# One graph layer on one core: another order of work in the head, the second round and the tail

## What is computed

```python
h = jnp.maximum(_layernorm(x, axis=-1), 0.0)
dep_emb = dep_emb_table[adj]
hi_t = h @ W1_w[:HID] + dep_emb @ W1_w[HID:] + W1_b      # rows i
hj_t = h @ W2_w[:HID] + dep_emb @ W2_w[HID:] + W2_b      # rows j
relevance = jnp.sum(hi_t * hj_t, axis=-1)
A = jax.nn.softmax(jnp.where(adj != 0, relevance, -1e9), axis=2)
h_syn = jax.nn.relu((A @ h) @ gcn_w + gcn_b)
return x + h_syn @ Wo_w + Wo_b
```

## Time and profile before

| | us |
|---|---|
| median of 3 runs | 360.76 (360.28 to 360.89) |
| the profiled execution | 359.88 |
| its span | 358.1 |
| PE busy | 346.7 |
| ACT busy, DVE busy, POOL busy | 264.9, 264.7, 175.2 |

### The profile page before, as it was taken

The page is one execution under the profiler, slowest core; times in us unless marked ns, Lnnn a source line. Parts: engine busy times, 40 slices in busy tenths (PEclk is TensorE's granted clock), DMA queues, the critical chain, the costliest instruction groups (busy, mean ns, idle before and its releaser), DMA issues.

```text
span 358.1 us, 9301 instructions
## 1 busy us (share of the span) xinstructions
PE 346.7 (97%) x3068; PEld 213.7 (60%) x3068; DVE 264.7 (74%) x664; ACT 264.9 (74%) x563; POOL 175.2 (49%) x354
## 2 busy tenths in 40 slices
PE   7999999899999999999999999999999999999985
PEld 6766565565657566565656566565756566565753
DVE  0998788686968777785968777695967777586664
ACT  2399896977787977778797877778697877755642
POOL 3067573756637182745638183745628183770000
PEclk9999999999999999999999999999999999999999
DMA  7994608965859395775759395675749383645052
GB/s 230 320 209 141 179 2 176 236 140 120 207 126 231 89 262 119 191 173 121 203 117 249 88 255 125 174 176 128 201 109 266 88 205 90 160 91 154 11 165 100
DMA packets 97000, 57.54 MB, mean 161 GB/s; under 512 B 60450, under 2 KB 96932, under 8 KB 96980
## 3 DMA queue, kind: packets, MB, share of 16 engines
q1 hardware_dynamic: 96272, 56.90, 63.8%
q10 hardware_dynamic: 644, 0.20, 0.3%
q0 software_dynamic: 64, 0.20, 0.2%
HBM read 17.44 MB, written 12.58 MB: 84 GB/s over the span
## 4 chain that ended last, share of the span: by engine, by line
PE 87%; DVE 4%; ACT 4%; DMA 2%; issue 1%; DVEq 0%; SPq 0%; ACTq 0%
PE bank L1174 24%; PE bank L1175 24%; PE bank L1176 24%; PE bank L1428 3%; PE bank L1423 3%; PE bank L1277 3%; PE bank L1285 2%; DMA x_all<-in_L_gnn_W_w_dram 2%; PE bank L1218 2%; ACT bank L652 1%; ACT h_tok L497 1%; PE bank L1488 1%; PE bank L1490 1%; ACT h_parts L497 1%; DVE bank L1069 0%
## 5 line engine op out<-in xcount | busy, mean ns | idle before, releaser
L449 POOL TENSOR_TENSOR h_parts<-h_tok,h_parts 128x1536 f16<-128x1536 f32 (+1 forms) x15 | 43.6, 2907 | 94.4 <-ACT h_parts L497 94.3
L1174 PE MATMUL bank<-gw_hi,hT 128*128 128x385 f16 x192 | 63.1, 328 | 1.6 <-DVE g_parts L924 1.1
L1176 PE MATMUL bank<-gw_hi,hT 128*128 128x385 f16 x192 | 62.7, 327 | 0.0
L425 POOL TENSOR_TENSOR x_all<-x_all,bo_all 128x1536 f32 (+1 forms) x16 | 55.0, 3442 | 15.7 <-ACT h_tok L515 15.7
L1175 PE MATMUL bank<-gw_lo,hT 128*128 128x385 f16 x192 | 62.6, 326 | 0.0
L924 DVE TENSOR_TENSOR g_parts<-bank,g_parts 128x512 f16<-128x512 f32 x48 | 33.2, 691 | 36.0 <-ACT bank L570 35.8
L1174 PE MATMUL bank<-wo_hi,z_hi 128*128 128x384 f16 x180 | 58.9, 327 | 0.5 <-DVE z_lo L1044 0.5
L1176 PE MATMUL bank<-wo_hi,z_lo 128*128 128x384 f16 x180 | 58.7, 326 | 0.0
L1175 PE MATMUL bank<-wo_lo,z_hi 128*128 128x384 f16 x180 | 58.7, 326 | 0.0
L1174 PE MATMUL bank<-hT,m_hi 128*128 128x512 f16 x144 | 54.6, 379 | 0.7 <-DVE hT L747 0.7
L1175 PE MATMUL bank<-hT,m_hi 128*128 128x512 f16 x144 | 54.6, 379 | 0.0
(11 more groups left out here) (165 smaller groups left out, 644.2 us busy)
## 6 DMA issues: line engine op xcount, KB each, us to landing
x_all<-in_x_dram SPq DMA_DIRECT2D x16, 768.0 KB, 6.9
out_dram<-x_all SPq DMA_DIRECT2D x15, 768.0 KB, 5.2
hg_parts<-hg_lo SPq DMA_DIRECT2D x32, 192.0 KB, 3.6
hg_parts<-hg_hi SPq DMA_DIRECT2D x32, 192.0 KB, 3.9
x_all<-in_L_gnn_W_w_dram SPq DMA_DIRECT2D x2, 576.0 KB, 5.2
out_dram<-x_all SPq DMA_DIRECT2D x4, 192.0 KB, 1.9
gcn_raw<-in_L_gnn_gcn_w_dram SPq DMA_DIRECT2D x1, 576.0 KB, 10.8
x_all<-in_L_gnn_Wo_w_dram SPq DMA_DIRECT2D x1, 576.0 KB, 11.5
```

Source lines behind the costliest of these rows:

```text
L425: nc.gpsimd.tensor_tensor(x_all[:, s, :, :], x_all[:, s, :, :], bo_all[:, :, :].broadcast_to([P, KT, D]), ALU.add).then_inc(x_biased, 1)
L449: ins = nc.gpsimd.tensor_tensor(h_parts[:, at, 1, :], h_tok[:, at, :], h_parts[:, at, 0, :], ALU.subtract)
L1174: nc.tensor.matmul(dst, lh, rh, start=(c == 0), stop=False)
L1176: last = nc.tensor.matmul(dst, ll, rh, start=False, stop=(c == DC - 1))
```

## The change

In the head:
- ACT copies W2 out of PSUM; before it was DVE.
- q is the 385th column in M's second and third chunk, so that one product with W1 (three matmuls) is left of two. The second chunk is made behind p and q and waits for q's copy; the bound's matmul stands behind the first matmul of the third chunk. DVE copies two columns out of M's banks.
- Three of four tiles of x(0) are normalised on DVE, one on ACT. The steps of M's scale on DVE stand one place earlier.
- gcn's bias is loaded through SP's queue behind gcn_w, before through ACT's. The broadcast of Wo's bias on POOL waits for W2.
- POOL works out x(1)'s coefficients before both bias passes, which follow one behind the other.

In the second round:
- ACT's three high parts of Wo stand behind the first move of scores, before one stood ahead of the transposed tiles. DVE's third low part of Wo stands ahead of the statistics of x(3).
- ACT splits hg's first tile between z's high part and its whole; rows are read from PSUM as soon as hg's tile is there (`row_of`), and the high parts of hg wait for them. On DVE hg's tiles 1 and 2 are split behind the two sums, tile 3 behind `exp_bias`.
- Output(1) on PE waits for z chunk by chunk.

In the tail:
- Scores go ahead of the fourth tile of hg. DVE builds three masks and a copy of the fourth's base (`last_masks`), and adds the fourth row's term to the scores later (`last_row`). The low parts of hg's tiles 2 and 3 follow `exp_bias`.
- The last attention is transposed ahead of the fourth output tile. Additions to the output of round 14 are spread: one, one, two.
- SP moves the last hg in six transfers with three waits (`move_last_hg`). The last aggregation does all products with `hg_parts` of a chunk first, then those with `hg_hi`.

The diff, cut to what the prediction speaks of:

```diff
+            def move_last_hg():
+                sp.wait_ge(z_done, DC * LAST)
+                sp.wait_ge(hg_split, KT * LAST + 2)
+                move_part(slice(0, S), hg_lo, slice(0, 2))
+                sp.wait_ge(hg_high, KT * (LAST + 1))
+                move_part(slice(S, 2 * S), hg_hi, slice(0, KT))
+                sp.wait_ge(hg_split, KT * (LAST + 1))
+                move_part(slice(0, S), hg_lo, slice(2, KT))
...
             sp.dma_start(gcn_raw[:, :, 0:D], gcn_w.rearrange("(c p) e -> p c e", p=P)).then_inc(gcn_loaded, 16)
+            sp.dma_start(gcn_raw[:, :, D:D + 1], gcn_b.rearrange("(c p o) -> p c o", p=P, o=1),
+                         allow_slow_non_contiguous=True).then_inc(gcn_b_loaded, 16)
...
+            pool.wait_ge(w2_loaded, 16)
             pool.dma_start(bo_all[:, 0, :], bo.partition_broadcast(P)).then_inc(bo_loaded, 16)
...
             add_bias(0)
-            make_bias(0)
             main_coefficients(1)
             pool.wait_ge(h_ready, 2 * KT * 2)
+            make_bias(0)
             make_bias(1)
...
+            for c in range(DC):
+                act.wait_ge(w_transposed, DC + c + 1)
+                nc.scalar.activation(w2T[:, c, 0:D], bank[DC + c][:, 0:D], ACT.Copy).then_inc(w2_copied, 1)
...
-            early_normalise(0, range(EARLY_WIDE, KT))
+            early_normalise(0, range(FIRST_WIDE, KT))
...
             def second_round():
-                wo_high_part(0)
                 for c in range(DC):
                     early_high_part(1, c)
                 move_scores(0, range(1))
-                wo_high_part(1)
-                wo_high_part(2)
+                for c in range(DC):
+                    wo_high_part(c)
...
-                z_parts(0, 0, bank[Z_BANK[0]][:, :])
+                z_high_part(0, 0, bank[Z_BANK[0]][:, :])
                 act.wait_ge(z_done, DC)
                 hg_high_part(1, 0)
-                z_parts(0, 1, bank[Z_BANK[1]][:, :])
-                z_parts(0, 2, bank[Z_BANK[2]][:, :])
+                z_whole(0, bank[Z_BANK[0]][:, :])
+                for c in range(1, DC):
+                    z_parts(0, c, bank[Z_BANK[c]][:, :])
+                move_scores(1, range(1))
                 for k in range(1, KT):
+                    act.wait_ge(row_ready, KT + k + 1)
                     hg_high_part(1, k)
-                move_scores(1)
+                move_scores(1, range(1, GT))
...
-            for c in range(DC):
-                dve.wait_ge(w_transposed, DC + c + 1)
-                nc.vector.tensor_copy(w2T[:, c, 0:D], bank[3 + c][:, 0:D]).then_inc(w2_copied, 1)
...
                 attention_high(1)
+                wo_low_part(2)
                 part_statistics(3, range(KT))
-                z_low_part(0, 0, bank[Z_BANK[0]][:, :])
                 rows_and_low(1, 0)
-                z_low_part(0, 1, bank[Z_BANK[1]][:, :])
-                wo_low_part(2)
-                z_low_part(0, 2, bank[Z_BANK[2]][:, :])
-                for k in range(1, KT):
-                    rows_and_low(1, k)
+                for c in range(DC):
+                    z_low_part(0, c, bank[Z_BANK[c]][:, :])
+                    dve.wait_ge(hg_done, KT + c + 2)
+                    row_of(1, c + 1)
                 dve.wait_ge(bias_made, 2)
-                scored_and_added(1)
+                all_masks(1)
+                summed_scores(1)
+                for k in range(1, DC):
+                    hg_low_part(1, k)
+                score_maxima(1)
+                hg_low_part(1, DC)
+                add_output(0, range(2))
+                attention(1)
+                add_output(0, range(2, KT))
...
+            def last_aggregated():
+                dve.wait_ge(hg_done, KT * LAST + DC)
+                row_of(LAST, 2)
+                last_masks()
+                z_low_part(LAST - 1, 2, bank[Z_BANK[2]][:, :])
+                masked_scores(LAST, last=True)
+                hg_low_part(LAST, 2)
+                hg_low_part(LAST, DC)
+                add_output(LAST - 1, range(1))
+                attention(LAST)
+                add_output(LAST - 1, range(1, 2))
...
-            pe.wait_ge(q_copied, 2)
+            pe.wait_ge(q_copied, 1)
             for c in range(DC):
-                last = m_step(2, c, D + 1)
+                last = m_step(1, c, D + 1)
             last.then_inc(m_done, 1)
+            m_step(2, 0, D + 1)
             pe.wait_ge(bound_ready, 1)
...
                 for k in range(KT):
+                    if last and k == DC:
+                        scored_supertile(s, half)
                     free_hg_tile(s, k, half)
```

More of the change, by code:

```diff
@@ L297, in move_hg, with move_part @@
                     sp.dma_start(hg_parts[S:2 * S, :, g, :], hg_hi[rows, :, :]).then_inc(hg_moved, 16)
+            def move_last_hg():
+                def move_part(lanes, part, tiles):
+                    for g in range(GT):
+                        sp.dma_start(hg_parts[lanes, tiles, g, :], part[g * S:(g + 1) * S, tiles, :])                          .then_inc(hg_moved, 16)
+                sp.wait_ge(z_done, DC * LAST)
[5 more added lines that the diff above has]
+                move_part(slice(0, S), hg_lo, slice(2, KT))
             sp.dma_start(w1_raw, W1[0:D, :].rearrange("(c p) e -> p c e", p=P)).then_inc(w1_loaded, 16)
@@ L656, in aggregated @@
             def aggregated(s):
+                last = isinstance(s, int) and s == LAST
                 for c in range(DC):
@@ L662, in aggregated @@
                         act.wait_ge(z_done, DC * s)
+                    if c == 2 and last:
+                        act.wait_ge(row_ready, KT * s + DC)
                     hg_high_part(s, c)
-                hg_high_part(s, DC)
+                if not last:
+                    hg_high_part(s, DC)
             def second_round():
-                wo_high_part(0)
                 for c in range(DC):
@@ L1060, in masked_scores, with last_masks, last_row, summed_scores @@
                                             None, ALU.add).then_inc(masked, 1)
+            def last_masks():
+                dve.wait_ge(row_ready, KT * LAST + DC)
+                for k in range(DC):
+                    nc.vector.tensor_scalar(masks[:, k, :], bias_all[:, KT * LAST + k, :], row_term[:, k:k + 1],
+                                            None, ALU.add).then_inc(masked, 1)
+                nc.vector.tensor_copy(masks[:, DC, :], bias_all[:, KT * LAST + DC, :]).then_inc(masked, 1)
+            def last_row():
+                dve.wait_ge(hg_done, KT * NSUP)
+                row_of(LAST, DC)
+                dve.wait_ge(row_ready, KT * NSUP)
+                dve.wait_ge(scored, LAST + 1)
+                nc.vector.tensor_scalar(scores[:, DC, :], scores[:, DC, :], row_term[:, DC:DC + 1], None,
+                                        ALU.add).then_inc(scored, 1)
+            def masked_scores(s, last=False):
+                if not last:
+                    all_masks(s)
+                summed_scores(s)
+                score_maxima(s, last)
+            def summed_scores(s):
                 dve.wait_ge(s_done, s + 1)
@@ L1156, in _ @@
             attention_high(2)
+            add_output(LAST - 1, range(2, KT))
             for c in range(DC):
@@ L1440, in output @@
                                   lambda e: (z_hi[:, e, rows], z_lo[:, e, rows]),
-                                  lambda e: (wo_hi[:, e, :], wo_lo[:, e, :])).then_inc(o_done, 1)
+                                  lambda e: (wo_hi[:, e, :], wo_lo[:, e, :]),
+                                  z_ready if first and k == 0 else None).then_inc(o_done, 1)
             def scored_supertile(s, half):
@@ L1503, in _ @@
             iteration(LAST, 1)
[L1504 to L1505 removed]
+            last_aggregation()
             last_output()
```

102 lines of the change are left out of this document (69 added, 33 removed).

## The result

The changed kernel takes **356.91 us** (median of 5 runs, 356.75 to 356.94) against 360.28 (360.23 to 360.89) for the kernel before in the same comparison: a ratio of 0.9901, 95% interval 0.9888 to 0.9915. Its profiled execution took 356.87 us, its span is 355.1.

A forecast was written before the change was run, and what follows sets the result against it. TensorE (PE) bounds the kernel, busy 346.7 of 358.1 us. Second round 1.0, which includes the head's gain, plus tail 1.0 make 2.0 off the 360.76 median: 358.7 us, range 357.3 to 360.0.

The forecast's parts named there:

- PE's own path: Head: fewer W1 products and no wait before x(0)'s transposes, against a new wait for q; PE gains 1.1 us.
- ACT decides what follows: Head, after PE's gain: ACT's passes over adj and its work on x(1) set when the second round starts.
- the 0.45 and the 0.33: Head, gains on ACT: adj passes start 0.45 us earlier, limited by adj's landing; the 0.33 wait for x(1)'s coefficients goes.
- the 0.52 for Wo's first part: Head, ACT: Wo's first part no longer stands ahead of x(1)'s transposed tiles, a gain of 0.52 us.
- the sum of 1.3: Head: DVE's first low part of x(1) comes 1.3 us earlier, so PE's second round starts at 36.7.
- The rival without a collision: Second round: POOL's subtraction starts behind DVE's `wo_lo`, DVE loses nothing, `exp_bias` gains 1.85; 357.9 us, chance 0.23.
- a late landing: Rival: adj 0.4 us late in the head or last hg parts 0.7 late in the tail; 359.2 to 359.9, chance 0.17.
- a late bias: Rival, head: Wo's bias lands late and delays x(1)'s coefficients on POOL; 361.7 us, slower than before, chance 0.05.
- POOL keeping its turn: Rival, second round: DVE waits for POOL's further casts and subtraction too, losing 2.6 us more; 361.3 us, chance 0.05.
- the collision: Second round: DVE's moved `wo_lo` meets POOL's subtraction and ends near 50.25 instead of 49.0; `exp_bias` still gains 1.0 us.
- the tail's term: Tail: scores ahead of hg's fourth tile and earlier transposes of the attention start the last aggregation 1.0 us earlier.
- The 0.4 and 1.3 of waits: Tail, PE's waits before the change, 1.3 of it for copies of the transposed attention; forecast to leave 0.75.

The follow-up runs named there:

- old_second_round: Changed kernel with the second round of DVE, ACT and PE as before, new head and tail kept: 356.49 us, ratio 0.9904.
- wo_behind_stats: Changed kernel with the second round's third `wo_lo` behind the statistics of x(3) instead of ahead: 356.51 us, ratio 0.9902.
- before_plus1: Kernel before plus one unused 1-column reciprocal on DVE, in idle time ahead of the last low parts of z: 359.43 us.
- lows_last: wo_behind_stats with low parts of hg tiles 1 and 2 of the second round behind row maxima and `exp_bias`: 355.36 us, ratio 0.9875.
- before_plus4: As before_plus1, but with four such reciprocals: 359.30 us.

## Why the prediction was right and where it was wrong

**Head: the number right, the path partly wrong.** PE's second round: forecast 36.7, measured 36.61 (36.48 to 36.99 over the kernels with this head). PE's own path was right in its sum: g(0) gained 1.06 of a forecast 1.1. The new wait for q ended at 12.66 (forecast 12.5), though not by the queue on DVE that I had made decisive. The statistics ahead of the copy started at 10.87 and were done at 11.9, and DVE then waited for PE's own products of q:

```profile
12.45 0.16 DVE L889 COPY x_all<-bank 128x3 f32<-128x3 f32 x1 [0.56 <-PE bank L1325]
```

"ACT decides what follows" failed. Adj's pass started at 21.73 (forecast 21.5) and the coefficients of x(1) stopped being waited for (ACT arrives at 31.76, they end at 31.48, forecast 31.1), and both helped the tokens to keep ahead of PE, which would have overtaken those of before (33.62 against 34.06). But PE waits for the tokens in neither kernel, so the 0.45 and the 0.33 are no terms of the time. PE's own 1.07 and 0.34 of the 0.52 for Wo's first part made 1.41. That the sum of 1.3 came near this is luck. So is part of adj's time: its load was issued 2.2 later than before (7.31 against 5.13), and landed after 14.3 instead of 16.4. That it would take 16.4 again was my estimate.

**Second round: right.** `wo_lo` took 1.75 from 47.09 (forecast 1.9 from 47.2), the wait before the fourth tile of hg 1.34 (1.6), masks at 53.54 (53.75), `exp_bias` ends at 57.53 (57.6), g(2) on PE at 65.98 (66.0). The rival without a collision did not come, nor a late landing, a late bias, or POOL keeping its turn. That the second round alone loses 0.3 was in the forecast's numbers, old_second_round confirmed it, and wo_behind_stats shows that the collision is the cause. That the moved `wo_lo` waits for POOL's whole subtraction was my estimate from the earlier trace rows, and it held: `wo_lo` ended at 48.84, 0.42 behind the subtraction (48.42), where the forecast had 50.25 behind 49.83. It doesn't hold for all that DVE does on SBUF alone: the statistics in the earlier trace rows took 1.94 beside POOL's subtraction.

**Wrong: the tail's term, 1.0 for 1.55.** The mechanism was right, its size was not, and the failed steps are two. First the chain on DVE: I put `exp_bias` 1.15 earlier, and it came 1.43 (2.49 - 1.06) earlier. Two of its steps I had put near the sum of their listed durations, and the next instruction starts before the listed end of the last:

```profile
335.42 0.21 DVE L967 TENSOR_SCALAR row_term<-bank,pq_scaled 128x1 f32<-128x1 f32 x1
335.66 0.58 DVE L1103 TENSOR_SCALAR masks<-adj_all,row_term 128x64 f32<-128x64 f32 x3
336.16 0.19 DVE L1105 COPY masks<-adj_all 128x64 f32<-128x64 f32 x1
336.26 0.68 DVE L1081 TENSOR_TENSOR z_lo<-bank,z_hi 128x512 f16<-128x512 f32 x1
336.86 0.89 DVE L1130 TENSOR_TENSOR bank<-bank,masks 64x256 f32<-64x256 f32 x2
```

From the end of tile 1's low part (335.51) to the end of the copy takes 0.84, where I had 1.03; the two sums end 0.81 behind z's low part, where I had 0.9. The other steps came within 0.04. That makes the 0.3. Second, the transposes: I gave PE 0.4 for four of them, the listed duration, but the output tile behind them starts after 0.23. That 0.17 is most of the other 0.2. The 0.4 and 1.3 of waits fell to 0.32 and 0, where I had left 0.75.

**Wrong: a term that was not in the sum, 0.39.** "The rest (z, output, stores) follows by the same steps" was the failed step. The row of before showed 1.53 of idle time ahead of the first addition (two matmul tiles instead of one), and I took it for the normal wait. It could have been seen: the addition started about when PE had finished two tiles of low products, though it needs one. before_plus1 shows that no order of work explains it; its cause stays open.

**Wrong: the base.** I took the sum off the median of three runs, 360.76, which was 0.88 above the profiled execution; later medians of before are 360.28, 359.90 and 359.98. With the profiled 359.88 as base the same sum gives 357.9. Of the 3.85 between 360.76 and 356.91, then, 2.0 was forecast, 0.07 came from head and second round beyond it, 0.55 from the tail, 0.39 from the late addition that only the kernel before has, and 0.84 was the base. The range, down to 357.3, had room for any one of the last three, not for all together.

## What to carry to other kernels

Add up starts, not durations: take the distance from one start to the next on the same engine in the old trace, because listed durations in two steps of a chain overstated it here by 0.3 us, and in four transposes by 0.17. A term that comes out right proves its path only if the waits on that path moved too: here ACT's tokens were made 1.0 earlier and PE waited for them neither before nor after, while the spread between executions followed the load of W2, for which PE did wait. After a reordering, look which instructions between the last input and the signal that others wait for are not needed for that signal; moving two of them behind it brought 1.04 (lows_last takes 19.24 from the start of the round to `exp_bias`, wo_behind_stats 20.28), while the whole new order of that round cost 0.35. And when a kernel is compared with a shifted version of itself, one instruction more can be worth 0.4 us, as in before_plus1: before a difference of that size is explained, compare milestones and look for idle time that no releaser accounts for.

## What the runs showed of the hardware that was not expected

An added 1-column instruction on DVE took 0.4 us off the span (358.0 to 357.6), where the first addition at the end starts 1.14 or 0.75 us behind the product. That the place of DVE's code is the reason is my reading of before_plus1 and before_plus4, and no run shows the mechanism. POOL's small instructions were slower beside DVE's `gw_lo`. While DVE makes the three (25.09 to 26.76 in the changed kernel), three of POOL's 4-column steps take 0.57 to 0.65, where one `gw_lo` takes 0.61:

```profile
24.95 0.21 POOL L379 TENSOR_TENSOR root_sq<-stats 128x4 f32<-128x4 f32 x1 [3.13 <-DVE stats L777]
25.11 0.65 POOL L379 TENSOR_TENSOR half_sum<-stats 128x4 f32<-128x4 f32 x1
25.71 0.57 POOL L379 TENSOR_TENSOR var_d<-stats 128x4 f32<-128x4 f32 x1
26.24 0.57 POOL L379 TENSOR_TENSOR root_sq<-root_sq 128x4 f32<-128x4 f32 x1
26.77 0.19 POOL L379 TENSOR_TENSOR half_sum<-half_sum,const_all 128x4 f32<-128x4 f32 x1
```

A step of 0.19 becomes 0.57 to 0.65, while the `gw_lo` take what a `wo_lo` of that shape takes at 52.73 in the earlier trace rows (0.61 each). The same steps for x(2), at 37.13 with no `gw_lo` beside them, take 0.20. In the kernel before, where the `gw_lo` run from 26.09, the steps from 26.41 take 0.39, 0.57 and 0.57, and 0.19 from then on. No experiment separates the two engines here: that the `gw_lo` are the cause is read from the times alone and not shown.
